# A Perceiver-like block of six layers: softmax weights divided on GpSimd ahead of their transposition, in place of transposed sums; another order and other first loads

## The reference, cut

```python
x = x + xattn0(layernorm(x), ctx, ctx, mask)      # 16 heads of 8, keys from ctx
x = x + attn0(layernorm(x))                        # causal, with a bias from "lines"
x = x + experts0(layernorm(x))                     # 8 experts, 2 of 4 groups, 2 picked
x = x + xattn1(layernorm(x), ctx, ctx)
x = x + attn1(layernorm(x))
x = x + experts1(layernorm(x))                     # 8 experts, 2 picked

# both cross-attentions
scores = einsum('bhqd,bhkd->bhqk', q, k) * scale   # 0: scores + where(mask == 0, -1e9, scores)
attn = softmax(scores, axis=-1)
ctx = einsum('bhqk,bhkd->bhqd', attn, v)
return ctx.transpose(0, 2, 1, 3).reshape(b, s, 128) @ Wo.T + bo
```

## Time and profile before

| | us |
|---|---|
| median of 3 runs | 1168.96 |
| lowest and highest | 1167.58, 1171.22 |
| the profiled execution | 1169.71 |
| its span, first to last instruction | 1168.0 |
| TensorE busy | 1098.4 |
| VectorE busy | 836.4 |
| ScalarE busy | 727.2 |
| GpSimd busy | 510.5 |

### The profile page before, as it was taken

How to read it: one execution, slowest core, us unless ns; L and a number is a source line. 1 busy time by engine, 2 the same in 40 slices (tenths; PEclk the granted TensorE clock), 3 DMA queues, 4 the chain that set the end, 5 groups by cost and what they waited for, 6 DMA issues and landing times.

```text
span 1168.0 us, 34915 instructions
## 1 busy us (share of the span) xinstructions
PE 1098.4 (94%) x13032; PEld 915.2 (78%) x13032; DVE 836.4 (72%) x2865; ACT 727.2 (62%) x2305; POOL 510.5 (44%) x712
## 2 busy tenths in 40 slices
PE   5987999999999999999999999999999999998898
PEld 3666778788888788787877878788888788877698
DVE  2666786678587685867868688686867766768685
ACT  3972636956666847667475674847757656555742
POOL 4485332464436444344444454344453534353430
PEclk9997899999999999999999999999999999999999
DMA  9620000100010010000000000110000000000000
GB/s 268 220 61 1 2 2 3 41 4 24 2 41 5 23 37 7 20 22 23 3 23 20 22 22 4 31 29 4 23 20 4 2 4 2 4 2 2 2 2 8
DMA packets 17732, 30.33 MB, mean 26 GB/s; under 512 B 2200, under 2 KB 14752, under 8 KB 16928
## 3 DMA queue, kind: packets, MB, share of 16 engines
q1 hardware_dynamic: 15264, 27.06, 7.7%
q10 hardware_dynamic: 2304, 1.05, 0.3%
HBM read 27.05 MB, written 1.05 MB: 24 GB/s over the span
## 4 chain that ended last, share of the span: by engine, by line
PE 63%; DVE 22%; ACT 5%; issue 4%; POOL 4%; DMA 1%; SPq 0%; DVEq 0%; POOLq 0%; ACTq 0%
PE bank L973 11%; PE bank L854 8%; PE bank L965 8%; PE bank L847 6%; PE bank L866 5%; PE bank L931 4%; PE bank L814 4%; PE bank L821 4%; DVE P L1298 2%; DVE P L1288 2%; PE bank L950 2%; DVE P L1291 2%; DVE xs L1308 2%; DVE cmp L1108 2%; ACT P L1013 1%
## 5 line engine op out<-in xcount | busy, mean ns | idle before, releaser
L965 PE MATMUL bank<-xnT,w 128*128 128x128 f32 x2048 | 256.9, 279 | 1.4 <-DVE P L1291 0.6
L965 PEld LDWEIGHTS bank<-xnT,w 128*128 128x128 f32 x2048 | 240.5, 193 | 10.4 <-issue 5.9
L1024 ACT COPY PT<-bank 128x512 f32<-128x512 f32 x256 | 147.4, 592 | 74.4 <-PE bank L854 72.2
L854 PE MATMUL bank<-cst,P 128*128 128x128 f32 x1024 | 151.0, 279 | 2.3 <-ACT P L1016 1.2
L1013 ACT ACTIVATE P<-P,nmax 128x257 f32<-128x257 f32 x256 | 132.0, 518 | 12.5 <-DVE nmax L1156 11.9
L1016 ACT ACTIVATE P<-bank,nmax 128x257 f32<-128x257 f32 x256 | 121.4, 485 | 24.9 <-DVE nmax L1160 24.4
L854 PEld LDWEIGHTS bank<-cst,P 128*128 128x128 f32 x1024 | 114.6, 142 | 27.0 <-issue 17.0
L1156 DVE CUSTOM_DVE_ANT_0 P<-bank,maskb,mscale 128x257 f32<-128x257 f32 x256 | 114.0, 480 | 29.5 <-PE bank L847 29.0
L973 PE MATMUL bank<-w2b,P 128*128 128x128 f32 x1024 | 132.7, 278 | 0.0
L973 PEld LDWEIGHTS bank<-w2b,P 128*128 128x128 f32 x1024 | 122.1, 192 | 6.5 <-issue 4.9
L1160 DVE TENSOR_REDUCE nmax<-bank 128x1 f32<-128x257 f32 x256 | 94.2, 415 | 35.9 <-PE bank L847 35.7
(11 more groups left out here) (133 smaller groups left out, 2208.2 us busy)
## 6 DMA issues: line engine op xcount, KB each, us to landing
ctxT<-ctx_in SPq DMA_DIRECT2D x16, 514.0 KB, 3.6
maskb<-mask_in SPq DMA_DIRECT2D x64, 128.5 KB, 2.8
w<-w_in SPq DMA_DIRECT2D x2, 2048.0 KB, 19.4
w2b<-w2b_in SPq DMA_DIRECT2D x1, 2048.0 KB, 27.4
wsq<-wsq_in SPq DMA_DIRECT2D x1, 1224.0 KB
xin<-x_in SPq DMA_DIRECT2D x16, 64.0 KB, 1.9
w2a<-w2a_in SPq DMA_DIRECT2D x1, 1024.0 KB, 19.2
out<-xs ACTq DMA_DIRECT2D x16, 64.0 KB, 1.5
```

Source lines behind the costliest of these rows:

```text
L854: ins = nc.tensor.transpose(ps[:, k * 128:k * 128 + 128], P[s][:, 2 * m + k // 2, (k % 2) * 128:(k % 2) * 128 + 128], ident)
L965: ins = nc.tensor.matmul(ps[:, k * 128:k * 128 + 128], wt[:, m, k * 128:k * 128 + 128], xnT[s][:, :], start=True, stop=True)
L1024: nc.scalar.copy(PT[:, place, m % 2 * 512:m % 2 * 512 + 512], ps[:, :]).then_inc(pt_done[s], 1)
```

## The change

The weights of a block are divided by their sums before they are transposed. A new step `scale` runs once for each batch b: VectorE takes the reciprocal of four sums when the block's four exponentials are done, and GpSimd multiplies the block's 4 x 256 weights in P by them, in place. `ptrans` waits for that. The 257th weights are multiplied by GpSimd as they are spread. `sel` and `rT` go, with their bank fill; `norm` with m = 0 multiplies On by the constant head mask, as it did with m = 1. On the start: bcol and the first three weight blocks (k0, v0, q0, which now stand first in wsq) come alone, then stream 0's context and x, then cst, and the other constants between stream 2's x and mask; `bo` becomes a step of the list with its own bank, and every engine waits for less. In the table durations are new, a change of product size costs TensorE `SWITCH` and counts with `STICK` in the choice of the next step, and all priorities are new.

```diff
-        "sel": ((DVE, .17), (POOL, 1.02)), "rT": ((PE, 4 * TR + .05),),
+        "scale": ((DVE, .19), (POOL, 2.1)), "norm": ((DVE, .6), (POOL, 1.32)),
...
-        "sscore": ((PE, .1 + .42 * (2 - l)), (DVE, 1.55 + .65 * l), (POOL, 1.03), (VACT, .54)),
+        "sscore": ((PE, .94 + .92 * (1 - l)), (DVE, 1.53 + .72 * l), (POOL, 1.05), (VACT, .53)),
...
-FIRST = {("mask", POOL): 17.0, ("kproj", PE): 13.0, ("ln", DVE): 14.0, ("xpb", POOL): 14.0, ("up", PE): 45.0}
-LATER = 6.0
+FIRST = {("kproj", PE): (4.8, 9.7, 13.6), ("ln", DVE): (5.2, 10.0, 13.9), ("xpb", POOL): (5.2, 10.0, 13.9),
+         ("mask", POOL): (7.9, 11.8, 19.5), ("bo", PE): (20.5,), ("up", PE): (30.0, 30.0, 30.0)}
+BEGIN = 4.0
...
         for b in range(GB):
+            add("scale", l, b, ("soft", l, NGR * b + NGR - 1, VACT))
             for w in (2 * b, 2 * b + 1):
-                add("ptrans", l, w, ("soft", l, 2 * w + 1, VACT))
+                add("ptrans", l, w, ("scale", l, b, POOL))
...
+                if pick_e == PE and kin[x] != was:
+                    v += SWITCH
+                key = v + (STICK if pick_e == PE and kin[x] != was else 0.0) - eager * prio[x]
...
-            for dst, src in ((cst[:, :], const_d), (bcol[:, :], bcol_d), (rows_in, brow_d[:, 0:512]),
-                             (router[:, :], brow_d[:, 512:520]), (wsq[:, :], wsq_d),
-                             (b2[:, :], b2_d)):
-                sp.dma_start(dst, src).then_inc(constants_in, 16)
+            for dst, src in ((bcol[:, :], bcol_d), (wsq[:, 0:WFIRST], wsq_d[:, 0:WFIRST])):
+                sp.dma_start(dst, src).then_inc(first_in, 16)
...
                 load_x(0, s)
+                if s == 0:
+                    sp.dma_start(cst[:, :], const_d).then_inc(constants_in, 16)
+                elif s == STREAMS - 1:
+                    for dst, src in ((wsq[:, WFIRST:WSQ], wsq_d[:, WFIRST:WSQ]), (rows_in, brow_d[:, 0:512]),
+                                     (router[:, :], brow_d[:, 512:520]), (b2[:, :], b2_d)):
+                        sp.dma_start(dst, src).then_inc(others_in, 16)
                 load_mask(0, s)
...
+                elif kind == "scale":
+
+                    pool.wait_ge(rsum_done[s], at(i, l, GB + 1, m + 1))
+                    u = slice(NGR * m, NGR * m + NGR)
+                    nc.gpsimd.tensor_tensor(P[s][:, u, 0:KM], P[s][:, u, 0:KM],
+                                            rsum[s][:, u].unsqueeze(2).broadcast_to((128, NGR, KM)),
+                                            ALU.mult).then_inc(scaled_done[s], 1)
...
-                    pe.wait_ge(exp_done[s], at(i, l, U, 2 * m + 2))
+                    pe.wait_ge(scaled_done[s], at(i, l, GB, m // 2 + 1))
...
-                elif kind == "rT":
-
-                    pe.wait_ge(wsel_done[s], at(i, l, 1, 1))
-                    for b in range(GB):
-                        ins = nc.tensor.transpose(
-                            ps[:, 128 * b:128 * b + 128],
-                            wsel[s][:, NGR * b:NGR * b + NGR, :, :], ident)
-                    ins.then_inc(full, 1)
...
+                elif kind == "scale":
+
+                    dve.wait_ge(exp_done[s], at(i, l, U, NGR * m + NGR))
+                    u = slice(NGR * m, NGR * m + NGR)
+                    nc.vector.reciprocal(rsum[s][:, u], sums[s][:, u]).then_inc(rsum_done[s], 1)
```

251 lines of the change are left out of this document (130 added, 121 removed).

## The result

| | before | after |
|---|---|---|
| median, us | 1169.47 (4 runs) | 1213.65 (4 runs) |
| lowest to highest | 1167.58 to 1171.22 | 1211.80 to 1215.82 |
| span of the profiled execution | 1168.0 | 1209.9 |
| mean granted clock in it | 0.987 | 0.961 |

The changed kernel is slower: its time is 1.0379 times that of before, interval 1.0354 to 1.0404. The forecast was 1150 us, from 1129 to 1171. The time lies above the range, and above even the highest figure of rival 1, 1199 us.

A forecast was written before the change was run, and what follows sets the result against it. TensorE, busy for 94% of the span, was taken to set the end. From the 1168.0 us span, -14.1 - 1.4 - 5.5 + 5 + 7 - 10 = -19.0 gave 1149.0, hence a time of 1150 us, range 1129 to 1171.

The forecast's parts named there:

- rival 1: Middle stretch: VectorE and GpSimd shut each other out, softmax and layer norm come late; 1174 to 1199 us, chance 0.13.
- transposes, spreads, size changes: On TensorE: 128 transposes of the sums gone, 14.1 us, and 16 fewer changes of product size, 1.4 us.
- start, new order: Ramp and middle stretch: earlier first loads save 5.5 us, the new four-engine order takes 10 us back.
- GpSimd's product is not hidden: Before a block's first transposition: longer wait for the weights' scaling, partly uncovered by other work; +5 us, bounds 0 and 21.
- VectorE is held: VectorE beside GpSimd's products: +69 us of stalls, +23 of reciprocals, a tenth reaching TensorE; +7 us, bounds 0 and +45.
- Rival 3: Middle, start and ramp: the order gives back more and the ramp's low clock does not return; 1129 us, chance 0.20.
- scale takes 2.9 us: GpSimd's new product: if it took this instead of 2.1 us, the sum would move towards rival 1 and Rival 2.
- Transposes: TensorE, line 883: 128 transposes of the sums at 0.11 us each removed, 14.1 us.
- The start: First loads: first projection at 6.5 us, 8.5 earlier; 5.5 us kept, bounds 0 and 8.5.
- The order: Middle stretch: the new order and table take back 10 of TensorE's 31 open us, bounds 0 and 20.
- xn at twice its mean: Layer norm on VectorE: a sign of rival 1, with comparisons also at twice their mean and TensorE's waits for VectorE grown.
- Rival 2: Ramp: GpSimd's added work binds it up to the first group's entry into layer 1; 1165 us, chance 0.12.

The follow-up runs named there:

- no_sums_old_order: Kernel before with the cross-attention's division by sums (transposes, spreads, reciprocals) left out, order and loads old: 1160.97 us, ratio 0.9951.
- short_product: Changed kernel with GpSimd's product cut from 4 x 256 to 4 x 4 numbers, weights left undivided: 1170.57 us, ratio 1.0008.
- power_product: Changed kernel with GpSimd's product replaced by a similarly long power of 128x10 numbers into its own tile, weights undivided: 1177.1 us, ratio 1.0089.
- xn_one_port_before: Kernel before with the layer norm's last step (xn) also writing a running sum: 1166.67 us, ratio 0.9997.
- product_by_scalar: Changed kernel with each GpSimd product as four instructions multiplying one tensor by one number a row: 1316.86 us, ratio 1.1278.
- sums_in_new_order: Changed kernel's planner, table and loads, with the transposed sums put back in place of the product: 1250.21 us, ratio 1.0709.

## Why the prediction was wrong, point by point

The whole, in the prediction's own terms. The measured column is the difference of two ratios, times 1168 us.

| term | predicted | measured | between |
|---|---|---|---|
| transposes, spreads, size changes | -15.5 | -5.7 | before, no_sums_old_order |
| start, new order | -5.5 - 10 | +6.7 | no_sums_old_order, short_product |
| GpSimd's product is not hidden | +5 | +9.5 | short_product, power_product |
| VectorE is held | +7 | +33.9 | power_product, after |
| sum | -19 | +44.3 | before, after |

**VectorE held: the step that failed most, by 27 us.** "I let a tenth of this through to TensorE", and the reason given was that VectorE has 26% open. The size of the stalls was overrated, not underrated: +69 us were forecast, +45 came (81.3 against 36.6), and VectorE's sum is 881 us, not 930. But two thirds of the hold came through: 34 us, for the 51 us of stalls that part power_product from the changed kernel (30.4 and 81.3). The share of open time, 26%, was no measure of what a queue in order lets through. It was named in rival 1, "no other work between", and then weighed by the average. The stalls of which the cost is shown are those in the chain from statistics to xn, where GpSimd delivers rstd and, with the next instruction of its queue, shuts VectorE out of using it: 96 instructions of xn alone were worth 11 us. Where the other 23 of the 34 come in stays open. And "of 37 us today hardly any reach TensorE" was right and no measure for the new ones: they lay for the most part beside instructions of 1.05 us and shorter, and xn_one_port_before shows that xn wasn't a narrow place then.

**The clock.** The sum had no term for it. Gaps of a few us, many of them behind a layer norm, were followed by stretches at 1.2 GHz, and these made some 30 us, about as much as the added idle time (26.0). Most of it comes with the new order and loads and not with the product's length: the stretches are 32.2 us before, 81.0 in short_product, 98.8 in power_product and 96.6 after. So in the table it lies mainly in the row of start and order, where it ate what the transposes gave. Rival 3 had priced the low clock of the ramp, but only as something that might go.

**The product** was put at 2.10 us from the earlier trace rows and is 1.90, 243 us in place of 269. That "scale takes 2.9 us" was out. Its size was right, and GpSimd's whole sum nearly so (732 against 760).

**GpSimd, not hidden.** +5 with bounds 0 and 21; 9.5 measured. The cover that was read from the order held for a product of 1.9 us: no long wait of line 877 for GpSimd, as foretold. product_by_scalar shows how near its end was: with 3.64 us in place of 1.90 the same order stands 149 us above the kernel before.

**Transposes.** 14.1 us was right as work and wrong as time. All of it was booked "on the engine that sets the end", at 94% busy. Taken out with nothing else changed, and the spreads with it, it gave 5.7 us (1.9 to 9.6 by the interval). That what stands after it is then late by its other inputs is argued from TensorE's idle time in that run.

**The start.** The first projection at 5.73 us against 6.5 forecast, even better. Its worth, 5.5 with a lower bound of 0, is at that bound: 0.9995. "Kept only as far as the data keep up" was the right sentence. The data in question are the second turn's masks behind 7 MB of weights, don't reach that far, and the chain of before had it: 6.99 us of DMA and 3.73 us of mask at 41 to 52 us.

**The order.** Of 31 open us 10 were to come back. Instead the new order, with the new loads, is 6.7 us worse than the old one with the sums taken out, even with the product cut short (128 products of 0.225 us, 96 more reciprocals and the longer tails are in that too). short_product has 12 stretches at 1.2 GHz, 81.0 us together, and no_sums_old_order has 5, 38.1 us. That the new order leaves its layer norms less cover is argued from the wait of 18.1 us for xn in short_product; which of its rules does it stays open, since sums_in_new_order couldn't tell.

**Rivals.** Rival 1 was what happened, with the right mechanism and a chance of 0.13. It gave 1174 at a third let through and 1199 at over half; at the two thirds that came through, by the same sum, it gives 1214 (1150 + 0.67 x 92 - 7 + 10). That this is the measured time is luck: the stalls were fewer, transposes and start gave less, and the clock was not in it. Its sign, xn at twice its mean, was half there (604 against 422 ns). Its place was wider than "the middle stretch". Rival 2, GpSimd binding the ramp, is there too: the gap at 41 us is worth 7 us beside the long products, and nothing that the times show beside the short one. Rival 3 was wrong.

## What to carry to other kernels

Price a long GpSimd instruction that reads two tensors by what VectorE can't start meanwhile, and look for the short VectorE step that a single chain hangs on; an open share of the engine's time was no cover for it here. Work taken off the busiest engine need not count in full (5.7 of 14 us here); take it out alone, before all else, to see. Look at an earlier first load by what it does to the last one of the ramp. And compare the granted clock of the variants: a new order can lose there what it saves in work.
